# The first round of a feed-forward layer: eight PSUM banks for its first task, four up products ahead of the down products, the third task's statistics earlier

## The reference

```python
x = x + attn_a(layernorm(x), gamma, w_qkva)   # q * scan over kv with sigmoid gates
x = x + ffn(layernorm(x), W1, b1, W2, b2)     # the layer of this change
x = x + attn_b(layernorm(x), W_q, W_k, W_v, W_o)
x = x + ffn(layernorm(x), W1, b1, W2, b2)

def ffn(x, W1, b1, W2, b2):                   # 256 -> 1024 -> 256
    h = gelu(einsum('bsd,fd->bsf', x, ternary(W1)) + b1)
    return einsum('bsf,df->bsd', h, ternary(W2)) + b2
```

## Time and profile before

| | |
|---|---|
| median of 3 runs | 1000.53 us (1000.41 to 1001.06) |
| the profiled execution | 1001.22 us, its span 999.5 us |
| PE busy | 976.4 us, 98% of the span |
| PEld busy | 889.9 us, 89% |
| DVE busy | 615.7 us, 62% |
| ACT busy | 487.2 us, 49% |
| POOL busy | 112.8 us, 11% |
| this feed-forward stage | 96.5 to 222 us on PE; the first round's down products begin at 112.27 |

### The profile page before, as it was taken

The page is one execution under the profiler, slowest core; times in us unless marked ns, Lnnn a source line. Parts: engine busy times, 40 slices in busy tenths (PEclk is TensorE's granted clock), DMA queues, the critical chain, the costliest instruction groups (busy, mean ns, idle before and its releaser), DMA issues.

```text
span 999.5 us, 41893 instructions
## 1 busy us (share of the span) xinstructions
PE 976.4 (98%) x18990; PEld 889.9 (89%) x18990; DVE 615.7 (62%) x1314; ACT 487.2 (49%) x941; POOL 112.8 (11%) x178
## 2 busy tenths in 40 slices
PE   8999899999999999999999999999999999999998
PEld 6888789999899999999998999899998998799997
DVE  6888877863446555455456644655545566667763
ACT  5676776643344433443353344343444335547663
POOL 2362322320000000000000000000000000112240
PEclk9999999999999999999999999999999999999999
DMA  9432112143323433343432442443343355322321
GB/s 324 137 83 85 64 64 85 65 148 107 121 75 118 148 122 108 129 130 108 130 109 93 155 140 72 133 142 108 109 130 129 108 159 164 114 90 74 127 75 53
DMA packets 76610, 115.84 MB, mean 116 GB/s; under 512 B 8848, under 2 KB 63504, under 8 KB 75408
## 3 DMA queue, kind: packets, MB, share of 16 engines
q1 hardware_dynamic: 76160, 113.15, 34.4%
q10 hardware_dynamic: 272, 0.00, 0.0%
HBM read 60.17 MB, written 52.95 MB: 113 GB/s over the span
## 4 chain that ended last, share of the span: by engine, by line
PE 93%; DVE 3%; issue 1%; ACT 1%; DMA 1%; POOL 0%; SPq 0%; POOLq 0%; DVEq 0%; ACTq 0%
PE bank L262 7%; PE bank L1269 6%; PE bank L264 6%; PE bank L263 6%; PE bank L1295 5%; PE bank L1280 4%; PE bank L1259 4%; PE bank L1329 4%; PE bank L1306 3%; PE bank L860 3%; PE bank L862 3%; PE bank L1377 3%; PE bank L1317 3%; PE bank L1378 3%; PE bank L1284 3%; PE bank L1260 3%
## 5 line engine op out<-in xcount | busy, mean ns | idle before, releaser
L1648 DVE STREAM_TRANSPOSE k<-kt 128x512 f32<-128x512 f32 x64 | 43.2, 694 | 101.2 <-ACT kt L1513 101.0
L1513 ACT COPY kt<-bank 128x512 f32<-128x512 f32 x64 | 37.6, 587 | 131.9 <-PE bank L264 131.9
L1676 DVE TENSOR_TENSOR ot_lo<-bank,ot_hi 128x512 fp32r<-128x512 f32 x64 | 41.2, 686 | 94.9 <-ACT ot_hi L1536 94.8
L1518 ACT COPY qt<-bank 128x512 f32<-128x512 f32 x64 | 37.5, 587 | 100.2 <-PE bank L264 100.2
L1523 ACT COPY v_all<-bank 128x512 f32<-128x512 f32 x64 | 37.5, 586 | 93.0 <-PE bank L1261 93.0
L262 PE MATMUL bank<-ln_xhi,wq_hi 128*128 128x256 f32 x256 | 73.8, 288 | 1.0 <-issue 1.0
L1329 PE MATMUL bank<-wo_hi,ot_hi 128*128 128x256 f32 x256 | 74.8, 292 | 0.0
L1280 PE MATMUL bank<-qt,state_s 64*64 64x64 f32 x2048 | 73.0, 221 | 1.5 <-issue 1.1
L1284 PE MATMUL bank<-qt,state_z 64*64 64x64 f32 x2048 | 73.1, 221 | 0.5 <-issue 0.5
L262 PE MATMUL bank<-ln_xhi,wk_hi 128*128 128x256 f32 x256 | 73.5, 287 | 0.0
L1280 PEld LDWEIGHTS bank<-qt,state_s 64*64 64x64 f32 x2048 | 66.2, 134 | 8.1 <-issue 2.3
(11 more groups left out here) (171 smaller groups left out, 2864.3 us busy)
## 6 DMA issues: line engine op xcount, KB each, us to landing
k_rows_scratch<-k SPq DMA_DIRECT2D x32, 512.0 KB, 3.4
k<-k_rows_scratch SPq DMA_DIRECT2D x128, 128.0 KB, 2.9
landed<-u_rows_scratch SPq DMA_DIRECT2D x124, 128.0 KB, 2.9
u_rows_scratch<-C_turned_u SPq DMA_DIRECT2D x30, 512.0 KB, 3.4
ln_xn<-x_rows_scratch SPq DMA_DIRECT2D x88, 128.0 KB, 3.0
x_rows_scratch<-B_turned SPq DMA_DIRECT2D x8, 512.0 KB, 2.6
x_rows_scratch<-C_turned SPq DMA_DIRECT2D x8, 512.0 KB, 4.0
xres<-in_L_attn_a_x_dram SPq DMA_DIRECT2D x7, 512.0 KB, 9.7
```

## The change

In the first round only, three things are ordered otherwise.

1. Tiles 4 to 7 of the first task go to the banks 6, 7, 4 and 5, which the down products use later. `h_bank` names them. So the first task has eight banks: its ups 4 and 5 wait for the last additions of line 690, ups 6 and 7 for the last low halves of line 229, and the second task's first four ups for lows 0 to 3 of the first.
2. In the second task four ups (`AHEAD`) come before the first down part, then two down parts and an up, one part and an up three times, and the last three parts. Before it was three ups, then one part and an up in turn, and three parts.
3. On DVE the statistics of the task (0, 1), which is the third one, stand in front of the last additions instead of behind low 1, and its normalisation behind low 1 instead of low 3. In the second task the high and low halves of the landed rows (lines 209 and 216) come one tile later, at f = 5 and f = 6.

The diff:

```diff
--- before.py
+++ after.py
@@ -771,7 +771,11 @@
             turned = place(f"{tag}_turned", 88, [P, 4, CH * DC, 32])
             n0 = NBLK
             HB, OB = (2, 3, 0, 1), ((4, 5), (6, 7))
-            LAG = 2
+            LAG, AHEAD = 2, 4
+
+            def h_bank(i, b, f):
+
+                return (*OB[1], *OB[0])[f - 4] if i + b == 0 and f > 3 else HB[f % 4]
 
             def steps(iteration, tail):
                 for i in range(NBLK):
@@ -835,12 +839,18 @@
                         pe.wait_ge(before.scan_done[1], START + DC * (NBLK - 1) + n + 1)
                     elif first and n == 2:
                         pe.wait_ge(before.wt_done, FC)
-                    if not first or n > 3:
+                    if first and 4 <= n < 6:
+                        pe.wait_ge(before.x_added[1], START + 2 * NBLK)
+                    elif first and 6 <= n < FC:
+                        pe.wait_ge(ln.low_done[1], START + (n0 + 1) * DC)
+                    elif first and FC <= n < FC + 4:
+                        pe.wait_ge(hlow_done, START + n - FC + 1)
+                    elif not first or n >= FC + 4:
                         pe.wait_ge(hlow_done, START + i * (2 * FC) + n - 3)
                     for k in range(DC):
                         w = w1t[:, k, f * P:(f + 1) * P]
-                        nc.tensor.matmul(bank[HB[f % 4]][:, :], w, ln.xhi[:, b, k, :], start=(k == 0), stop=False)
-                        last = nc.tensor.matmul(bank[HB[f % 4]][:, :], w, ln.xlo[:, b, k, :],
+                        nc.tensor.matmul(bank[h_bank(i, b, f)][:, :], w, ln.xhi[:, b, k, :], start=(k == 0), stop=False)
+                        last = nc.tensor.matmul(bank[h_bank(i, b, f)][:, :], w, ln.xlo[:, b, k, :],
                                                 start=False, stop=(k == DC - 1))
                     last.then_inc(h_ready, 1)
 
@@ -866,14 +876,19 @@
 
                 def iteration(i, first, last):
                     for b in range(B):
-                        behind = former(b, i, first)
+                        behind, parts = former(b, i, first), 0
                         for f in range(FC):
+                            if first and b:
+                                for part in range(2 if f == AHEAD else 1 if f > AHEAD else 0):
+                                    down(*behind, parts)
+                                    parts += 1
                             up(b, i, f, first)
-                            if behind and f >= LAG:
-                                down(*behind, f - LAG)
+                            if behind and f >= LAG and not first:
+                                down(*behind, parts)
+                                parts += 1
                             if first and b == 0 and f == 1:
                                 last_turns()
-                        for part in range(FC - LAG, FC if behind else 0):
+                        for part in range(parts, FC if behind else 0):
                             down(*behind, part)
 
                 def tail():
@@ -885,7 +900,7 @@
             def scalar(act, last_high):
                 def high(b, i, f):
                     act.wait_ge(gelu_done, START + i * (2 * FC) + b * FC + f + 1)
-                    nc.scalar.copy(hid_hi[:, b, f, :], bank[HB[f % 4]][:, :]).then_inc(hhigh_done, 1)
+                    nc.scalar.copy(hid_hi[:, b, f, :], bank[h_bank(i, b, f)][:, :]).then_inc(hhigh_done, 1)
 
                 def iteration(i, first, last):
                     for b in range(B):
@@ -896,13 +911,13 @@
                         for f in range(FC):
                             n = b * FC + f
                             act.wait_ge(h_ready, START + i * (2 * FC) + n + 1)
-                            nc.scalar.activation(bank[HB[f % 4]][:, :], bank[HB[f % 4]][:, :], ACT.Gelu,
+                            nc.scalar.activation(bank[h_bank(i, b, f)][:, :], bank[h_bank(i, b, f)][:, :], ACT.Gelu,
                                                  bias=b1_sb[:, f:f + 1]).then_inc(gelu_done, 1)
                             if f:
                                 high(b, i, f - 1)
                             if first and b == 0 and f == 1:
                                 last_high()
-                            if target and f == 4:
+                            if target and f == (5 if first else 4):
                                 ln.act_high_rows(act, target[0], moves(target[0], target[1] - 1))
                         high(b, i, FC - 1)
 
@@ -930,14 +945,17 @@
                         dve.wait_ge(out_ready[b], START + i * 2)
                         if first and b == 0:
                             dve.wait_ge(before.split_low, 16)
+                            dve.wait_ge(before.x_added[b], START + 4)
+                            dve.wait_ge(before.shift_done[b], NBLK + 1)
+                            ln.dve_statistics(dve, b, 1, n0 + 1)
                             last_rows()
                         for f in range(FC):
                             dve.wait_ge(hhigh_done, START + i * (2 * FC) + b * FC + f + 1)
-                            nc.vector.tensor_tensor(hid_lo[:, b, f, :], bank[HB[f % 4]][:, :],
+                            nc.vector.tensor_tensor(hid_lo[:, b, f, :], bank[h_bank(i, b, f)][:, :],
                                                     hid_hi[:, b, f, :].bitcast(FP32), ALU.subtract).then_inc(hlow_done, 1)
                             if first and b == 0 and f == 0:
                                 last_low()
-                            if f == 1:
+                            if f == 1 and not (first and b == 0):
 
                                 if last:
                                     dve.wait_ge(x_added[b], START + 2)
@@ -946,13 +964,13 @@
                                 if first:
                                     dve.wait_ge(before.shift_done[b], NBLK + 1)
                                 ln.dve_statistics(dve, b, 0 if last else i + 1, n0 + i + 1)
-                            if f == 3:
+                            if f == (1 if first and b == 0 else 3):
                                 dve.wait_ge(ln.rstd_done[b], START + n0 + i + 2)
                                 ln.dve_normalise(dve, b, 0 if last else i + 1, n0 + i + 1, ln_rstd)
                             if f == 4:
                                 dve.wait_ge(ln.normalised[b], START + (n0 + i + 2) * CH)
                                 ln.dve_turn(dve, b, turned, moves(b, i))
-                            if target and f == 5:
+                            if target and f == (6 if first else 5):
                                 ln.dve_low_rows(dve, target[0], target[2])
                             if behind and f == 5:
                                 add_rows(*behind, 0)
```

## The result

The changed kernel took 998.35 us in the median of 7 runs (996.86 to 999.74), the kernel before 1000.64 (1000.32 to 1002.27). The ratio is 0.9976 with an interval of 0.9965 to 0.9987: 2.4 us less, between 1.3 and 3.5 (both by the ratio). The forecast was 997.5 in a range of 996.7 to 998.9, faster with a chance of 0.84. The profiled execution took 998.16 us, its span 996.4; 998.2 and 996.5 were forecast.

The account below looks back on a forecast made before the run. PE was taken to bound the kernel, losing 3.8 us waiting at DVE's pace. A gain of 3.57 us less 0.55 given back is 3.02, so 1000.53 falls to 997.5 us, range 996.7 to 998.9.

Parts of the forecast that it names:

- Banks: First round on PE: ups 4 to 11 run through without waiting, and the first down part counts as started at 109.62.
- The four waits for low halves: PE's up products waiting on DVE's low halves between 95 and 150 us: 2.8 us in 4 times.
- 12.16 - 8.28: PE before the change: time from up 2 to the first down part, less nine ups at 0.92; called 3.8 us lost.
- Statistics in idle time: On DVE, the third task's statistics start at 98.00, before 99.61, and end at 99.73, when the additions start.
- Line 216 is late next: DVE's low halves of the next round's rows start at 120.08, take 1.28 us undisturbed and end at 121.36.
- the give-back: At the next round's first up, PE waits for line 216 until 121.49, which gives back 0.55 us.
- the 120.94 of the forecast: Time at which PE is done with the round's down parts and ups and ready for the next round's first up.
- 3.57: Full gain in us on PE at the next round's first up, 120.94 against 124.51, before the give-back.
- hidden, by little: Turned rows' trip through memory takes 7.6 us at most and is over by 115.3, before ACT wants them at 115.6.
- the forecast 115.6: Time at which ACT wants the landed rows, behind the gelu of up 13 and a copy.
- number 2: Line 216 still takes 1.54, or DVE is late at lows 5 to 7; gain 2.0 to 2.76 us; chance 0.16.
- rival 4: Slower: ACT waits for landed rows; delay free up to 0.6 us, doubled trip bound gives 1004.2 us; chance 0.04.

Follow-up runs that it names:

- trip started late: Changed kernel with the third task's turned rows saved only when the eighth low half is done; 999.26 us in one execution.
- the kernel with 2.06 us: Changed kernel with the third task's statistics and normalisation where they were before; 1001.20 us against 1001.20, ratio 0.9992.

## Why the prediction was right

Points 1 to 3 hold to a tenth or so, each taken from the same starting up 2.

1. Banks: forecast 9.38 us from up 2 to the end of low 7 (100.11 to 109.49), and 9.51 to the first down part, its slower first matmul included; measured 9.40 (99.96 to 109.36), and this matmul was 0.10 slower than the ones behind it. The four waits for low halves are gone. The loss before was 12.16 - 8.28 = 3.9 us, not the 3.8 that the prediction says, but nothing in its sum uses that.
2. Statistics in idle time: forecast from 98.00, additions at 99.73; measured 97.85 and 99.58. Less the 0.15 us by which this execution was early, these are the same numbers, and low 7 is 0.04 off (109.49 forecast as the end, 109.30 measured).
3. Line 216 is late next, and undisturbed: 1.28 forecast, 1.28 measured. The rule of the Trainium skill, SBUF — State Buffer, section "Who interferes with whom", gave the same.
4. The mis-sized term is the give-back at the next round's first up, forecast 0.55 us. The last matmul of the down product started at 120.67 and such matmuls step by 0.12, so the up could have started at 120.79: the 120.94 of the forecast less 0.15. It started at 121.61, 0.82 later, and its first matmul took 0.11 longer, which makes 0.93 us. 3.57 - 0.93 = 2.64, and the stage shows 2.60. What was wrong is the trip of the turned rows, which I had "hidden, by little". From the turn's end (107.53) to ACT it took 8.7 us, not at most 7.6. Counted from the same up 2, ACT took the rows 0.76 us behind the forecast 115.6, and low 14 and line 216 came 0.34 late. A delay was to cost nothing up to 0.6 us; in four profiles delays of 0.76, 0.48, 0.51 and (trip started late) 1.49 us made line 216 0.34, 0.05, 0.09 and 1.06 late, so the slack was about 0.4.
5. The sum, 3.0 us: the stage shows 2.6 to 2.9, the timed ratios 2.3 to 3.0. Of rivals, number 2 (a larger give-back, 997.8 to 998.5) names the measured median better than the forecast, though by another cause than I gave it; 0.1 us of the difference is that the kernel before took 1000.64 in seven runs and 1000.53 in the three that I started from. That the profiled execution hit its forecast so closely (998.16, 998.2 forecast) is luck: its stage gave 2.60 of the 3.0 us, and up 2 0.15 earlier and 0.6 less in the stretch behind it (604.2 to 603.6), which the change doesn't touch, did the rest.

Why the trip was long, the packet records tell in part. My bound was an upper one for the trip as it was, not for a trip at another moment, and against rival 4 I had said that nothing else moves beside it. But two transfers on the instruction queues fall in this time. In the kernel before they start at the ends of the trip's two halves: 8 KB at 112.06, with the save's last packet, and 16 KB at 116.18, with that of the loads. In the changed kernel the 8 KB start at 109.47, inside the save (packets from 108.38 to 110.34), and the 16 KB at 113.47, inside the loads (111.77 to 115.74). The save's packets then reach over 1.96 us and not 1.51, those of the loads over 3.97 and not 2.73. The loads are the larger part. All thirteen profiles fit:

| | inside | outside |
|---|---|---|
| 8 KB transfer and the save: first to last packet | 1.96 to 1.98 us (7 profiles) | 1.42 to 1.51 (6) |
| 16 KB transfer and the loads: first to last packet | 3.66 to 3.97 (9) | 2.56 to 2.73 (3), 3.26 (1, started 0.14 us ahead) |

With eight banks and four ups ahead alone, the 8 KB came ahead of the save and the 16 KB inside the loads; the save was short and the loads were long, so each goes with its own transfer. It stays a coincidence in time, seen each time; no experiment separated it.

What the prediction missed is how the parts combine. Taken apart they do -1.65 (statistics) and -0.95 us (banks and four ups), which happen to add up to the whole of -2.60; but the banks alone do +2.05. They gather PE's four short stops into one of 3.0 us, and the clock falls in it. The fourth up ahead fills 0.9 us of this hole and the earlier statistics nearly all of the rest.

## What to carry to other kernels

Closing several short waits may open one long one, in which the clock falls: here one of 3.0 us cost more than four with 3.9 us in all. Look at the longest hole and not only at the sum, and fill it or split it. When a bottleneck's input comes early, walk the next hand-over instruction by instruction: here the low halves of the next task's rows cost 0.6 to 1.0 us of the stage only for standing one tile too late in DVE's order. A transfer that was hidden with tenths to spare need not be hidden once its start moves: other transfers, those of the instruction queues among them, don't move with it.

## What was not expected of the hardware

- On PE an idle time of 3.01 us was accompanied and followed by a granted clock of 0.50 for 6.8 us, at a price of 2.7 us of the stage. Idle times of 2.06 and 1.17 us in the same place, and four of up to 1.11, were not in their profiles; but a fall also came 1.1 us behind an idle time of 1.68 us elsewhere, and 4 of 10 timed executions of the kernel with 2.06 us have a mean clock of 0.998. So no safe length of a hole can be read from these runs.
- Two DVE operations with both inputs in SBUF took 1.28 us alone and 2.15 beside GpSimd's additions, which took 3.71 instead of 2.83.
- The same save of 512 KB took 2.6 to 2.7 us to landing, or 3.2 to 3.3 where an 8 KB transfer of an instruction queue fell inside it; the packets of the loads reached over 2.6 to 2.7 us, or 3.7 to 4.0 with a 16 KB one inside.
